# A transformer stack on one core: row-tiled attention scores, a shared tail tile, and a different split of the normalisations

## What is computed

```
h   = shift_token(x)                       # the upper 128 channels come from the token before
q, k, v = split(h @ wqkv)                  # 8 heads of 64
q, k = rotary_xpos(l2norm(q)*qs, l2norm(k)*ks)
att = softmax(8 * q k^T, window: own 128-block and the one before it) @ v
x   = x + att @ wo
h   = layernorm(shift_token(x)) * lg + lb
a, g = split(h @ w1 + b1)                  # 2 x 682 columns
x   = x + (a * gelu(g)) @ w2 + b2
```

## Time and profile before

| | us |
|---|---|
| median of three runs | 847.18 |
| the profiled execution's own time | 846.62 |
| its span, first to last instruction | 844.8 |
| PE busy / DVE busy / ACT busy / POOL busy | 759.1 / 569.6 / 502.4 / 441.6 |

### The profile page before, as it was taken

How to read it: one execution, slowest core, us unless ns; L and a number is a source line. 1 busy time by engine, 2 the same in 40 slices (tenths; PEclk the granted TensorE clock), 3 DMA queues, 4 the chain that set the end, 5 groups by cost and what they waited for, 6 DMA issues and landing times. The chain is left out here.

```text
span 844.8 us, 17684 instructions
## 1 busy us (share of the span) xinstructions
PE 759.1 (90%) x5088; PEld 652.9 (77%) x5088; DVE 569.6 (67%) x1675; ACT 502.4 (59%) x1241; POOL 441.6 (52%) x625
## 2 busy tenths in 40 slices
PE   5988777989999999999998988999999999999977
PEld 4877655887878787878786877878787878787856
DVE  2798896385858584848485856757575858585842
ACT  2333436366767666666667573757575757575742
POOL 1333464373838383838383645737373737373722
PEclk9999987799999999999999998999999999999999
DMA  7344323151000000000000001010101010101000
GB/s 212 128 137 149 110 57 131 26 219 37 3 29 9 29 8 26 12 20 17 19 18 19 20 2 50 2 51 0 50 0 50 0 50 0 50 0 37 1 26 13
DMA packets 31156, 38.34 MB, mean 45 GB/s; under 512 B 7356, under 2 KB 21776, under 8 KB 31120
## 3 DMA queue, kind: packets, MB, share of 16 engines
q1 hardware_dynamic: 31120, 37.90, 14.0%
HBM read 29.51 MB, written 8.39 MB: 45 GB/s over the span
## 5 line engine op out<-in xcount | busy, mean ns | idle before, releaser
L1351 POOL TENSOR_SCALAR pr<-pr,rl 128x128 f32<-128x128 f32 (+1 forms) x256 | 106.4, 429 | 96.9 <-DVE rl L1129 96.8
L840 ACT ACTIVATE pr<-sm,nb,rn 128x128 f32<-128x128 f32 (+1 forms) x256 | 137.3, 539 | 19.3 <-DVE nb L1124 19.2
L415 PE MATMUL ps<-hT_hi,w_hi 128*128 128x256 f32 (+1 forms) x384 | 110.9, 289 | 1.4 <-DVE hT_lo L1091 1.4
L1120 DVE CUSTOM_DVE_ANT_0 sm<-ps,wmask 128x128 f32<-128x128 f32 (+1 forms) x256 | 81.4, 355 | 41.6 <-PE ps L581 23.0
L415 PE MATMUL ps<-hT_hi,w_lo 128*128 128x256 f32 (+1 forms) x384 | 108.3, 282 | 0.0
L415 PE MATMUL ps<-hT_lo,w_hi 128*128 128x256 f32 (+1 forms) x384 | 107.9, 281 | 0.0
L1314 POOL TENSOR_TENSOR rn<-ss,nhalf 128x16 f32<-128x16 f32 x32 | 95.3, 2978 | 3.7 <-POOL ss L1310 2.0
L798 ACT ACTIVATE sqb<-ps 128x512 f32<-128x512 f32 x64 | 38.2, 598 | 84.9 <-PE ps L415 84.9
L415 PE MATMUL ps<-wqkv_hi,yT_hi 128*128 128x512 f32 x192 | 79.8, 416 | 8.7 <-DVE arena L967 5.3
L1257 POOL TENSOR_SCALAR hrs<-hmv 128x2 f32<-128x2 f32 x16 | 3.1, 193 | 151.7 <-DVE hmv L1145 151.7
L809 ACT ACTIVATE gl<-ps,b_sb 128x256 f32<-128x256 f32 x96 | 45.5, 474 | 53.3 <-PE ps L415 52.9
(11 more groups left out here) (146 smaller groups left out, 2209.2 us busy)
## 6 DMA issues: line engine op xcount, KB each, us to landing
arena<-x SPq DMA_DIRECT2D x16, 256.0 KB, 3.6
ystream<-arena SPq DMA_DIRECT2D x16, 256.0 KB, 2.0
y_next<-ystream SPq DMA_DIRECT2D x16, 256.0 KB, 2.9
y_res<-ystream SPq DMA_DIRECT2D x16, 256.0 KB, 2.6
arena<-L_ffn_w SPq DMA_DIRECT2D x2, 1364.0 KB
arena<-ctx SPq DMA_DIRECT2D x8, 256.0 KB, 4.1
arena<-mask_BxSxS_ik SPq DMA_DIRECT2D x8, 256.0 KB, 2.9
xmid<-arena SPq DMA_DIRECT2D x8, 256.0 KB, 2.0
```

The lines of the kernel that those rows point to most:

```text
L415: last = mm(out, lhsT(a), rhs(b), start=(start and i == 0), stop=(stop and i == 2))
L840: A(pr[:, h % NS, a:b], sm[:, h % NS, a:b], ACT.Exp, bias=nb[:, h, t:t + 1], scale=rn8[:, t, h:h + 1], accum_out=ls[:, h, t:t + 1]).then_i ...
L1120: V.tensor_tensor_reduce(sm[:, h % NS, a:b], bank(h % NS)[:, a:b], wmask[:, a:b], 1.0, NEG, ALU.add, ALU.max, mx[:, h, t:t + 1]).then_inc( ...
L1351: G.tensor_scalar(pr[:, h % NS, a:b], pr[:, h % NS, a:b], rl[:, h, t:t + 1], 1.0, ALU.mult, ALU.mult).then_inc(pn_done, 1)
```

## The change

It makes these edits.

- **Scores.** The queries' transposes go into `qT`, a tile without zero padding, in one ACT instruction. The scores of a pair of heads are four matmuls with 64 contraction rows, head 2p on rows 0 to 63 and head 2p+1 on rows 64 to 127 of the array. Pair 0 is issued before the five downs, pairs 1, 2, 3 in the loop at h = 0, 1, 3. `sm` and `pr` get four buffers, the score banks stay three. The zeroing of `qz` goes.
- **Norms.** The tables hold the factor -8, the mask has the opposite sign, `row_max` becomes `row_min`. DVE multiplies queries and keys by their inverse norms in one instruction over 1024 columns (`scale_heads`), for tile 1 after one sum over 1024 columns (`add_both`). `nb`, `rn8`, `nrn8` go, and the exponential has the constant scale -1. `tr_heads(t,0)` waits for `ks_done` in place of `sum_done`; the place of `tr_heads` in PE's order is not changed.
- **Tail.** The two 42-row tiles of the last up share one stationary tile of 106 columns, its second half at column 64: six matmuls in place of 12. `w1` is loaded with four DMAs in place of one for that; the b1 of the tail moves to partition 64 and its sum becomes two instructions.
- **Rows.** `normalise_rows` moves from DVE to ACT (scale and bias from POOL, which gets two more small instructions); it stands between the squares of tile 1.
- **Order.** PE: `project(1,(0,1))` before `project(0,(2,))` and before the transposes of `hn`. ACT and DVE: see the diff.

```diff
-    NS = 3
+    NS, SB = 4, 3
...
+            def up_parts(c):
+                if c < HC - 1:
+                    return [(c * P, P, 0), (HF + c * P, P, 1)]
+                return [(2 * HF, GT + HT, 0)]
...
-                    pe.wait_ge((sum_done, ks_done)[j], T * s + t + 1)
+                    if j == 0:
+                        pe.wait_ge(ks_done, T * s + t + 1)
...
+                def scores_own(pair):
+                    for h in (2 * pair, 2 * pair + 1):
+                        if h >= SB:
+                            pe.wait_ge(mn_done, T * (HEADS * s + h - SB + 1))
+                    for h in (2 * pair, 2 * pair + 1):
+                        r = slice(h % 2 * DH, h % 2 * DH + DH)
+                        mm(bank(h % SB)[:, 0:P], qT[r, pair, 0:P], kT[r, pair, 0:P], start=True, stop=True)
+                def scores_both(pair):
+                    for h in (2 * pair, 2 * pair + 1):
+                        r = slice(h % 2 * DH, h % 2 * DH + DH)
+                        mm(bank(h % SB)[:, P:3 * P], qT[r, pair, P:S], kT[r, pair, :], start=True, stop=True)\
+                            .then_inc(s_mm2, 1)
...
+                    project(1, (0, 1))
                     project(0, (2,))
                 if first:
                     weigh_values(NB - 1)
-                if A:
-                    project(1, (0,))
                 if F:
                     pe.wait_ge(hn_done, s)
                     transpose_rows(hn, 7).then_inc(h_tr, 1)
                 if A:
-                    project(1, (1, 2))
+                    project(1, (2,))
...
-                    pe.wait_ge(q_done, 2 * T * s + 2)
+                    pe.wait_ge(q_done, T * s + 1)
                     pe.wait_ge(k_done, T * s + 1)
                     pe.wait_ge(v_done, T * (s + 1))
-                    for h in range(NS):
-                        scores_own(h)
-                    pe.wait_ge(q_done, 2 * T * (s + 1))
+                    scores_own(0)
+                    pe.wait_ge(q_done, T * (s + 1))
                     pe.wait_ge(k_done, T * (s + 1))
-                    for h in range(NS):
-                        scores_both(h)
+                    scores_both(0)
...
-                        if h + NS < HEADS:
-                            scores_own(h + NS)
-                            scores_both(h + NS)
+                        if h in (0, 1, 3):
+                            scores_own((h + 3) // 2)
+                            scores_both((h + 3) // 2)
...
+                    if c < HC - 1:
+                        A(gl[:, c % 2, :], ps[:, 5 + c % 2, S:2 * S], ACT.Gelu,
+                          bias=b1_sb[:, lf, 1, c:c + 1]).then_inc(gl_done, 1)
+                    else:
+                        A(gl[0:r, c % 2, :], ps[GT:GT + r, 5 + c % 2, 0:S], ACT.Gelu,
+                          bias=b1_sb[GT:GT + r, lf, 1, c:c + 1]).then_inc(gl_done, 1)
...
-                    q = qz[:].rearrange("p (c j) n -> p c j n", j=2)
-                    for j in range(2):
-                        lo = j * DH
-                        A(q[lo:lo + DH, :, j, t * P:(t + 1) * P],
-                          ps[lo:lo + DH, i, :].rearrange("p (c n) -> p c n", c=PAIRS), ACT.Copy)\
-                            .then_inc(q_done, 1)
...
+                    A(qT[:, :, t * P:(t + 1) * P], bank(i).rearrange("p (c n) -> p c n", c=PAIRS),
+                      ACT.Copy).then_inc(q_done, 1)
...
-                        A(pr[:, h % NS, a:b], sm[:, h % NS, a:b], ACT.Exp, bias=nb[:, h, t:t + 1],
-                          scale=rn8[:, t, h:h + 1], accum_out=ls[:, h, t:t + 1]).then_inc(e_done, 1)
+                        A(pr[:, h % NS, a:b], sm[:, h % NS, a:b], ACT.Exp, bias=mn[:, h, t:t + 1],
+                          scale=-1.0, accum_out=ls[:, h, t:t + 1]).then_inc(e_done, 1)
...
+                def normalise_rows():
+                    act.wait_ge(sh_mm, s)
+                    act.wait_ge(hshift_done, s)
+                    wait(act, h_tr, f)
+                    wait(act, u_done, HC * f)
+                    for t in range(T):
+                        for i, half in enumerate((x1[:, t, 0:P], bank(7)[:, t * P:(t + 1) * P])):
+                            last = A(hn[:, t, i * P:(i + 1) * P], half, ACT.Identity,
+                                     bias=hmr[:, t:t + 1], scale=hrs[:, t:t + 1])
+                    last.then_inc(hn_done, 1)
                 if la is not None:
                     squares(0, 0)
                     squares(0, 1)
+                    squares(1, 0)
+                if lf is not None:
+                    normalise_rows()
+                if la is not None:
+                    squares(1, 1)
                     values(0)
                 if lf is not None:
                     act.wait_ge(h_tr, s)
                     wait(act, up_mm, HC * f)
                     A(hT[0][:], halves(7), ACT.Copy).then_inc(hT_high, 1)
                 if la is not None:
-                    squares(1, 0)
-                    squares(1, 1)
+                    values(1)
                 if lf is not None:
                     gelu(0)
-                if la is not None:
-                    values(1)
-                if lf is not None:
                     gelu(1)
                     high_u(0)
...
-                def add_keys(t):
-                    V.tensor_tensor(t1[:, t, INNER:2 * INNER], t1[:, t, INNER:2 * INNER],
-                                    t2[:, INNER:2 * INNER], ALU.add).then_inc(ksum_done, 1)
...
+                def add_both(t):
+                    dve.wait_ge(rot_done, T * s + t + 1)
+                    V.tensor_tensor(t1[:, t, :], t1[:, t, :], t2, ALU.add).then_inc(sum_done, 1)
+                def scale_heads(t):
+                    dve.wait_ge(sum_done, T * s + t + 1)
+                    if t == 0:
+                        dve.wait_ge(ksum_done, s + 1)
+                    heads = t1[:, t, :].rearrange("p (h d) -> p h d", d=DH)
+                    by = rn[:, t, :].unsqueeze(2).to_broadcast([P, 2 * HEADS, DH])
+                    V.tensor_tensor(heads, heads, by, ALU.mult).then_inc(ks_done, 1)
...
+                def row_min(h):
-                               (nb_done, HEADS * s))
+                               (e_done, T * (HEADS * s + max(0, h - NS + 1))))
-                                               NEG, ALU.add, ALU.max, mx[:, h, t:t + 1]).then_inc(mx_done, 1)
-                    dve.wait_ge(mx_done, T * (HEADS * s + h + 1))
-                    dve.wait_ge(rn8_done, 2 * T * (s + 1))
-                    V.tensor_tensor(nb[:, h, :], mx[:, h, :], nrn8[:, :, h], ALU.mult).then_inc(nb_done, 1)
+                        V.tensor_tensor_reduce(sm[:, h % NS, a:b], bank(h % SB)[:, a:b], wmask[:, a:b], 1.0,
+                                               -NEG, ALU.add, ALU.min, mn[:, h, t:t + 1]).then_inc(mn_done, 1)
...
-                if F:
-                    normalise_rows()
                 if start:
                     dve.wait_ge(w_ready, FIRST)
                 if A:
                     rotate_cos(0)
+                    rotate_sin(0)
                 if F:
                     low_hT()
                 if A:
-                    rotate_sin(0)
-                    add_queries(0)
-                if A:
                     norms(1, 0)
                     norms(1, 1)
+                    add_queries(0)
+                    rotate_cos(1)
                 if F:
                     gated(0)
                 if A:
-                    scale_keys(0)
+                    rotate_sin(1)
+                    scale_heads(0)
                 if F:
                     gated(1)
                 if A:
-                    rotate_cos(1)
+                    add_both(1)
                 if F:
                     gated(2)
                 if A:
-                    rotate_sin(1)
+                    scale_heads(1)
                 if F:
                     gated(3)
...
-                if A:
-                    add_queries(1)
-                    add_keys(1)
-                if A:
-                    scale_keys(1)
...
-                    wait(pool, e_done, T * HEADS * s)
+                    wait(pool, ks_done, T * s)
...
-                def score_scales(t):
-                    G.tensor_scalar(rn8[:, t, :], rn[:, t, 0:HEADS], QK_SCALE, 1.0, ALU.mult, ALU.mult)\
-                        .then_inc(rn8_done, 1)
-                    G.tensor_scalar(nrn8[:, t, :], rn[:, t, 0:HEADS], -QK_SCALE, 1.0, ALU.mult, ALU.mult)\
-                        .then_inc(rn8_done, 1)
...
+                    G.tensor_scalar(hmr[:], hmv[:, :, 0], -1.0, 1.0, ALU.mult, ALU.mult).then_inc(hneg_done, 1)
+                    pool.wait_ge(hrstd, s)
+                    pool.wait_ge(hneg_done, s)
+                    G.tensor_tensor(hmr[:], hmr[:], hrs[:], ALU.mult).then_inc(hshift_done, 1)
-                    score_scales(0)
-                if la is not None:
-                    score_scales(1)
...
```

(29 more changed lines are left out.)

91 lines of the change are left out of this document (38 added, 53 removed).

## The result

The changed kernel takes 873.0 us (median of 4 runs, 871.2 to 875.0) beside 847.2 before (median of 4): a ratio of 1.031 with a 95% interval of 1.029 to 1.033, so it is slower, as forecast, and inside the range. The profiled execution took 871.19 us, its span is 869.4.

A forecast was written before the change was run, and what follows sets the result against it. PE's timeline was taken as the bound, sharing the limit with ACT's chain in the head loop. From 846.6 us, +15 for 15 longer steps and +8 for five clock falls gave 870 us, range 853 to 888 (0.8).

The forecast's parts named there:

- The stall at the last value product: PE waits for ACT's copy of tile 0's values, which use the same bank: a new stall of 0.5 us.
- The wait at the first head transposes: At tr_heads(0,0) PE, there at 617.3, idles 2.6 us until DVE's scale_heads(0) is done at 619.9.
- The idle at 624.63: PE's old 0.76 us wait for DVE's scaled keys, before the head transposes of tile 1, goes.
- First exponentials: In ACT's head loop the first exponential comes 1.3 us later, the third, head 2's first, 1.5 later.
- Exponential and scores: Constant scale saves 0.09 us per exponential, counted as 0.6 a step; a score pair takes 0.85 side by side, not 1.30.
- Tail: Six matmuls of 256 columns go from the last up, on PE's path: a gain of 0.71 us a step.
- The clock: After PE's long idle the clock halves for 3.4 us, costing 1.7 each, in five steps: +8 us; bounds none to 12.
- The rest: Step 0, step 16 and the missing zeroing, put at 0 together, bounds -2 and +3 us.
- The rule against the change: DVE instructions with two SBUF inputs and GpSimd's SBUF reads exclude each other; scale_heads(0) would begin at 619.2: +0.5 a step.
- The rival of 878: GpSimd's power of tile 1 holds DVE's scaling: 878 us, chance 0.04.
- No falls: The granted clock does not fall after PE's long idle: 862 us, chance 0.20.
- The faster one: Tile 0's scaled heads are ready before PE arrives, DVE's queue being shorter than summed: 822 us; faster had chance 0.10.

The follow-up runs named there:

- experiment 9: experiment 4 with tile 0's value product and its copy earlier, DVE's query sum between tile 1's norms, pair 1's scores among the downs: 811.3 us, 0.957.
- Experiment 3: The changed kernel with tr_heads(0,0) and tr_heads(0,1) each one up later on PE, ACT's copies after them, DVE's order kept: 840.8 us, 0.992.
- experiments 5: The changed kernel with the exponential's scale read from a 128x1 tile of -1.0 in place of the constant: 874.9 us, 1.032.
- experiment 6: experiment 4 with the exponential's scale read from a 128x1 tile in place of the constant: 833.4 us, 0.984.
- Experiment 7: experiment 4 with scores over 128 rows on zero-padded queries again, the queries copied in two pieces: 851.3 us, 1.005.
- Experiment 1: The changed kernel with twenty unused 256-column matmuls on PE between up(1) and the first head transposes: 861.2 us, 1.016.
- experiment 4: The changed kernel, tile 0's head transposes each one up later; DVE's norms and query sum ahead of low_hT, tile 1's rotations ahead of gated(0): 825.1 us, 0.973.
- experiment 8: experiment 4 with the six 256-column matmuls of the shared tail issued twice: 837.9 us, 0.988.
- experiment 2: The changed kernel with only DVE's order altered, tile 1's norms and add_queries(0) ahead of low_hT: 881.8 us, 1.040.

## Why the prediction was right

870 was forecast, 873.0 came; the profiled execution, on which the sum was made, took 871.2. The steps, in the order of the prediction:

- **The stall at the last value product.** 0.5 from 612.42 to 613.0 was forecast. The transposes of `hn` start at 612.07 (257.07 + 355.0; 612.06 forecast), and the product at 613.0. From start to start that is 0.93, where experiment 9 has 0.36 without a wait: a stall of 0.57. (The row shows 0.33 of it as idle, since durations overlap.) Right.
- **The wait at the first head transposes, the largest term.** `low_hT` was put at 613.47 and starts at 613.47; the scaling at 618.7, starts at 618.75. PE resumes at 620.11, not 619.9: the hand-over from DVE to PE, 0.14 from 264.97 to 265.11, wasn't in the sum. The wait is 2.57 in the row (2.5 forecast) and stands in every step with both parts, with 2.1 in one. Experiment 3 shows that it is the wait that makes the change slower: with the places of two transposes and of ACT's copies alone changed, it shrinks to 0.74 and the same kernel is 0.8% faster than before.
- **The idle at 624.63 goes.** It has gone; the transposes of tile 1 follow without a gap.
- **First exponentials.** +1.3 and +1.5 were forecast. The first starts at 274.64, or 629.6, which is 1.6 behind the 628.02 that it had before; that of head 2 waits 0.92 for the row minimum and starts at 277.43, or 632.4, 1.85 behind the 630.58 that it had before. Both are 0.3 more than forecast. For head 2, 0.2 of it is there already at the transposes of tile 1 (625.98; 625.75 forecast). For the first, the sum left out the load of the exponential's table. It ends at 274.61, while the row minimum is there at 274.26:

```profile
272.89 0.42 ACT L831 ACTIVATE u_hi<-u_pair 128x256 fp32r<-128x256 f32 x1
273.33 1.28 ACT L852 ACT_TABLE_LOAD   x1
274.64 0.40 ACT L852 ACTIVATE pr<-sm,mn 128x128 f32<-128x128 f32 x1
```

- **Exponential and scores.** -0.6 was counted for the one; experiments 5 and 6 show 0.6 and 0.67. The pair of scores was taken as 0.85. In the timeline the 128-column part of a pair and its 256-column part follow at 275.60 and 275.93 and the four wide ones are busy 0.60, where two untiled ones of that width were busy 0.60 in the earlier trace rows; so the two of a pair run beside each other: 0.33 for the narrow ones and some 0.5 for the wide ones, from start to start. The 0.2 in it for entering and leaving the mode was a figure without a row; the pair of heads 6 and 7 takes 0.85 in all, from 281.34 to the transposes at 282.19. Experiment 7 leaves 0.78 a step for it.
- **Tail.** 0.71 was forecast, 0.63 is what issuing it again costs.
- **Sum of a step:** +0.9 to +1.0 forecast, +1.1 measured (43.59 against 42.45), 17 us where 15 stood. With the 1.85 of head 2 in place of 1.5 the prediction's own sum would give 1.2; the hand-over of 0.14 is a part of that.
- **The clock.** Five falls at 1.7 were taken. Seven came, each 3.41 us at 0.50 as in the earlier trace rows, and each costs 1.35 (44.94, the mean of the two, less 43.59): 9.5 us. The 1.7 was too high because PE isn't dense through the fall: it begins at 219.63, while PE stands idle until 220.21, and the row of that stretch has PE busy 2.83 of the 3.41, half of which is 1.4. Experiment 1 puts 11.8 on all of them. The bounds of none and twelve falls held the seven; that five at 1.7 (8.5) come near seven at 1.35 (9.5) is in part luck, since the two errors offset each other. With the 17 us it makes 26.5 where the middle stretch shows 25.4.
- **The rest** was put at 0: the two ends measure -3.6 and +2.8. In the last stretch PE waits up to 4.8 us for the rows normalised on ACT, where the longest such wait on DVE was 3.8. What shortened the first stretch wasn't tried, and it may be no effect of the change: the kernels of experiments 4 and 8 have the same instructions in it, and their profiles differ by 4.2 there (157.8 and 162.0).

**One thing in its steps was wrong without harm.** The prediction let "copying queries in one piece" gain nothing, since it lies beside the ups. That is so only while the transposes behind it wait 0.76 for DVE. That wait is gone after the change, and experiment 7 shows that the second piece then costs 0.70 a step (in kernel 4's order). The cover was there, but the same change took it away.

**The rule against the change.** The scaling starts at 263.75, and the power of tile 1 runs to 264.08, as POOL's timeline shows:

```profile
261.16 2.92 POOL L1323 TENSOR_TENSOR rn<-ss,nhalf 128x16 f32<-128x16 f32 x1
264.06 1.50 POOL L1334 TENSOR_TENSOR u_lo<-u_pair,u_hi 128x256 fp32r<-128x256 f32 x1
```

So the scaling began 0.33 us inside the power and took 1.22, the same as undisturbed. The low part behind it took 1.50, where it takes 0.72 to 0.74 when nothing holds it, and ended 0.59 after the scaling: that one waited for the scaling. The Trainium skill (SBUF — State Buffer, Who interferes with whom) has either hold the other off; the low part agrees, here and in experiment 2 in the other direction, the power again does not. The rival of 878 falls.

**The rivals.** No falls (862) did not come by itself; it is what experiment 1 makes, at 861. The faster one (822, if the scaled heads were ready before PE) is experiment 4, at 825: the mechanism is real, and the order of the queues decides which side one is on. Serial tiles, a long exponential and many falls did not come.

## What to carry to other kernels

When an edit hangs a transfer of work on a later result, ask what stands ahead of that result in its engine's queue, and move the consumer and the producer together with it: here 48 us lay between two orders of the same instructions. Cost an edit at nothing only after you have asked whether another part of it removes the cover. A gain in busy time on every engine says little while one wait grows.

## What was not expected of the hardware

- An idle of one length is not followed by one clock. Behind 2.57 to 2.58 us the granted clock fell to 0.50 for 3.41 us in nearly every second step of 43.6 to 45.0 us; in experiment 5, with the same 2.57 and steps of 44.20, steps 2 to 6 have none. No run here settles what decides it. That kernel, with 0.6 more in each step, is so only 1.9 us slower in all.
- Twenty matmuls without a purpose made a kernel 11.8 us faster.
- Who starts first decides who is held. With DVE's scaling 0.31 us ahead of POOL's low part they took 1.22 and 1.50; with the low part 0.32 ahead (experiment 2), 1.48 and 0.72.
